# First merge stage: normalizers inverted as 8 columns a tile and spread over head dimensions on TensorE

## The reference

```
q = elu(q) + 1                                   # nodes x 8 x 64
k = elu(k) + 1
kv = einsum('bhnd,bhne->bhde', k, v)             # one 64x64 matrix a head
k_sum = sum(k over nodes)                        # one vector of 64 a head
out = einsum('bhnd,bhde->bhne', q, kv)
normalizer = einsum('bhnd,bhd->bhn', q, k_sum)   # one number a node and head
out = out / (normalizer[..., None] + 1e-8)
out = out.reshape(B, N, C) @ out_w.T + out_b
```

## Time and profile before

| what | value |
|---|---|
| time of the kernel, median of 3 runs | 4578.88 us (4555.28 to 4579.88) |
| span of the profiled execution | 4670.9 us |
| time outside that span | not shown by the profile |
| PE busy in the whole span | 4108.2 us (88%) |
| DVE busy | 3416.2 us (73%) |
| ACT busy | 2670.2 us (57%) |
| POOL busy | 2813.0 us (60%) |
| stage `merge0` | 1736 to 1960 us |

### The profile page before, as it was taken

One profiled execution on the slowest core, in us unless ns is written; L12 is line 12 of the kernel. 1 busy time (PEld: TensorE's weight loads), 2 busy tenths in 40 slices (PEclk: granted clock), 3 DMA queues, 4 the chain that ended last, 5 costly groups with the idle time before them and its releaser, 6 DMA issues. The chain is left out here.

```text
span 4670.9 us, 65873 instructions
## 1 busy us (share of the span) xinstructions
PE 4108.2 (88%) x16821; PEld 2295.3 (49%) x16821; DVE 3416.2 (73%) x9304; ACT 2670.2 (57%) x7162; POOL 2813.0 (60%) x2738
## 2 busy tenths in 40 slices
PE   7888888999999989979775889988889999999967
PEld 3344554555555545456454444444445555555543
DVE  8521226999999987667653888888888888888873
ACT  1111115888888871123254777777777777777720
POOL 1766664777777761013422777777777777777700
PEclk9988989999999999979887999999999999999978
DMA  4224115888888861257667999999999999988853
GB/s 178 89 96 138 37 37 179 255 257 256 252 256 255 253 214 59 83 190 232 194 210 248 223 223 225 221 228 225 223 230 222 222 224 222 224 218 217 181 167 134
DMA packets 368712, 910.65 MB, mean 195 GB/s; under 512 B 60879, under 2 KB 113086, under 8 KB 368089
## 3 DMA queue, kind: packets, MB, share of 16 engines
q0 software_dynamic: 209424, 663.87, 53.7%
q1 hardware_dynamic: 148287, 222.61, 14.4%
q10 hardware_dynamic: 10650, 20.19, 1.2%
HBM read 679.00 MB, written 227.92 MB: 194 GB/s over the span
## 5 line engine op out<-in xcount | busy, mean ns | idle before, releaser
L2126 POOL DMA_INDIRECT mid_acc<-m_out,m_il x416 | 688.4, 1655 | 149.9 <-issue 117.6
L2522 PE MATMUL m_pws<-m_w_s,m_hid 32*128 32x512 f32 x832 | 472.4, 650 | 138.9 <-DVE m_msg L2202 78.2
L2116 POOL DMA_INDIRECT m_drow<-mid_drow,m_ig x416 | 421.4, 1013 | 262.0 <-DMA m_ig<-in_gather_ix 111.8
L441 POOL DMA_INDIRECT mid_slots<-sort_rec,f_row x416 | 412.3, 991 | 264.8 <-issue 112.3
L807 POOL DMA_INDIRECT s_kv<-mid_kv_rows,keep_slot x440 | 425.9, 968 | 209.8 <-PE s_pm L1034 124.8
L1034 PE MATMUL s_pm<-s_kv,keep_free 128*128 128x260 f32 x1760 | 466.2, 388 | 47.5 <-ACT s_kv L951 37.5
L2530 PE MATMUL m_pm<-m_msg,m_same 128*128 128x512 f32 x832 | 491.4, 674 | 11.5 <-ACT m_out L2352 8.8
L2415 PEld LDWEIGHTS m_pip<-keep_ident,m_drow 128*128 128x128 f32 x2496 | 368.7, 204 | 246.3 <-issue 235.8
L2116 POOL DMA_INDIRECT m_srow<-mid_srow,m_ig x416 | 404.1, 971 | 126.9 <-issue 126.3
L2523 PE MATMUL m_pwf<-m_w_f,m_hid_f 32*128 32x512 f32 x832 | 476.7, 655 | 0.0
L1015 PE MATMUL s_pq<-queries_q,s_sameT 128*128 x880 | 467.8, 614 | 0.1
(11 more groups left out here) (396 smaller groups left out, 8619.1 us busy)
## 6 DMA issues: line engine op xcount, KB each, us to landing
mid_ys<-e_y SPq DMA_DIRECT2D x57, 256.0 KB
e_line<-in_src_lines POOLq DMA_DIRECT2D x52, 256.0 KB
m_line<-in_src_lines SPq DMA_DIRECT2D x104, 128.0 KB
m_xT<-mid_xhT SPq DMA_DIRECT2D x100, 128.0 KB
g_a<-mid_acc SPq DMA_DIRECT2D x50, 256.0 KB, 3.4
keep_w<-in_w SPq DMA_DIRECT2D x16, 512.0 KB
s_kv<-mid_kv_rows,keep_slot POOLq DMA_INDIRECT x440
mid_slots<-sort_rec,f_row POOLq DMA_INDIRECT x416
```

The lines of the kernel that those rows point to most:

```text
L441: pool.indirect_dma_start(io["slots"], bass.IndirectOffsetOnAxis(ap=sort.row[:, e:e + 1], axis=0), sort.rec[:, e, :], None,).then_inc(s_pu ...
L2116: pool.indirect_dma_start(row, None, table, bass.IndirectOffsetOnAxis(ap=ig[:, n, t:t + 1], axis=0),).then_inc(s_g[t % S], 16)
L2126: pool.indirect_dma_start(io["acc1"][k % NACC], bass.IndirectOffsetOnAxis(ap=il[:, t:t + 1], axis=0), out[:, k % R, :], None, compute_op=A ...
L2522: pe.matmul(pws[k % 2][:], hid[lanes, par, :], w_s2[lanes, :], start=True, stop=True)
```

## The change

- `keep.ksum` is now 2 columns a chunk, one for each head, instead of 128. VectorE writes it with 128x2 instructions.
- `head_sums` has its operands the other way round: q (128x128) is loaded and the 2 columns of `ksum` stream. The result is one number a node and head, nodes on the partitions: 8 columns a tile.
- ScalarE copies 8 columns, and VectorE inverts 8 columns (`inverses`).
- New is `spread_heads`: 8 products a tile. For head h, the column of inverses is loaded, repeated 64 times (128x64), and the identity streams with 128 columns. The result goes to 64 partitions of PSUM bank `pk`, partitions 0 to 63 for even h and 64 to 127 for odd h, turned as q is.
- VectorE multiplies q by that PSUM bank.
- Head sums, their copy and the inverses run two tiles ahead instead of one. Those of tiles 0 and 1 come before the folding. The spreading of tile 0 follows the folding and waits for all four copies of `kvw`; that of tile n+1 stands between the products of tile n with W and those with `kvw`.

```diff
-                    vec.tensor_tensor(keep.ksum[:, c, :].rearrange("p (h d) -> p h d", h=2),
-                                      pkv[:, c, P:P + 1].unsqueeze(2).broadcast_to([P, 2, DH]), over_dims(half), ALU.mult)
+                    vec.tensor_tensor(keep.ksum[:, c, :], pkv[:, c, P:P + 1].broadcast_to([P, 2]), half[:], ALU.mult)
...
 def head_sums(pe, q, ksum, bank):
     for c in range(KC):
-        cols = slice(P * c, P * (c + 1))
-        ins = pe.matmul(bank[:, cols], ksum[:, c, :], q[:, cols], start=True, stop=True)
+        ins = pe.matmul(bank[:, 2 * c:2 * c + 2], q[:, P * c:P * (c + 1)], ksum[:, c, :], start=True, stop=True)
+    return ins
+
+def spread_heads(pe, z, ident, bank):
+    for h in range(H):
+        rows, cols = slice(DH * (h % 2), DH * (h % 2 + 1)), slice(P * (h // 2), P * (h // 2 + 1))
+        ins = pe.matmul(bank[rows, cols], z[:, h:h + 1].broadcast_to([P, DH]), ident[:], start=True, stop=True)
     return ins
...
-        z, zq = s.sb("z", [P, 2, H]), s.sb("zq", [P, 2, D])
+        z, zq = s.sb("z", [P, 2, H]), s.sb("zq", [P, 2, H])
...
 # VectorE
-                def divide_queries(i, j):
-                    n = U * i + j
+                def inverses(n):
                     vec.wait_ge(s_zq, n + 1)
                     vec.reciprocal(zq[:, n % 2, :], zq[:, n % 2, :]).then_inc(s_rq, 1)
-                    vec.wait_ge(s_rq, n + 1)
-                    vec.tensor_tensor(q[:, j, :], q[:, j, :], zq[:, n % 2, :], ALU.mult).then_inc(s_q, 1)
+
+                def divide_queries(n):
+                    vec.wait_ge(s_spread, n + 1)
+                    vec.tensor_tensor(q[:, n % U, :], q[:, n % U, :], pk[n % 2][:], ALU.mult).then_inc(s_q, 1)
...
                 norm_edges(0, 0)
+                inverses(0)
+                inverses(1)
                 norm_edges(0, 1)
-                divide_queries(0, 0)
+                divide_queries(0)
 ...
-                        if not (isinstance(n, int) and n + 2 >= NT):
+                        if n + 2 < NT:
+                            inverses(n + 2)
                             norm_edges(i + (j + 2) // U, (j + 2) % U)
                         if not last_tile(n):
-                            divide_queries(i + (j + 1) // U, (j + 1) % U)
+                            divide_queries(n + 1)
                         add(i, j)
...
 # ScalarE
-                    need(act, s_q, n - 1)
-                    act.activation(zq[:, n % 2, :], pn[n % 2][:], ACT.Copy, bias=1e-8).then_inc(s_zq, 1)
+                    need(act, s_spread, n - 1)
+                    act.activation(zq[:, n % 2, :], pn[n % 2][:, 0:H], ACT.Copy, bias=1e-8).then_inc(s_zq, 1)
...
 # TensorE
+                def spread(n):
+                    pe.wait_ge(s_rq, n + 1)
+                    pe.wait_ge(s_kvw, KC)
+                    need(pe, s_q, n - 1)
+                    spread_heads(pe, zq[:, n % 2, :], keep.ident, pk[n % 2]).then_inc(s_spread, 1)
...
-                sums(0, 0)
+                sums(0)
+                sums(1)
                 turn(0, 0)
...
                     pe.matmul(pk[c % 2][:], kvT[:, P * c:P * (c + 1)], w_out[:, c, :], start=True, stop=True).then_inc(s_kw, 1)
+                spread(0)
...
+                        if n + 2 < NT:
+                            sums(n + 2)
                         if not last_tile(n):
-                            sums(*nxt)
                             turn(*nxt)
                         pe.wait_ge(s_aT, n + 1)
                         need(pe, s_x, n - 1)
                         for c in range(KC):
                             pe.matmul(pout[n % 2][:], aT[:, j, P * c:P * (c + 1)], W[:, c, :], start=c == 0, stop=False)
+                        if not last_tile(n):
+                            spread(n + 1)
                         pe.wait_ge(s_q, n + 1)
-                        if n == 0:
-                            pe.wait_ge(s_kvw, KC)
```

More of the change, by code:

```diff
@@ L1103, in merge0 @@
         s_back = [s.sem(f"x_back{j}") for j in range(U)]
-        s_st, s_agg, s_pn, s_zq, s_rq, s_q, s_ta, s_aT, s_mm, s_x = (s.sem(n) for n in (
-            "edge_steps", "edges", "head_sums", "normalizers", "inverses", "queries", "edgesT", "aT", "products", "x"))
+        s_st, s_agg, s_pn, s_zq, s_rq, s_spread, s_q, s_ta, s_aT, s_mm, s_x = (s.sem(n) for n in (
+            "edge_steps", "edges", "head_sums", "normalizers", "inverses", "inverses_spread", "queries", "edgesT", "aT", "products", "x"))
         s_kv, s_kvT, s_kw, s_kvw = (s.sem(n) for n in ("kv_turned", "kvT", "folded", "folded_weights"))
@@ L1185, in _, with normalizers @@
                 act.dma_start(W[:], io["w_ff"].rearrange("(c p) n -> p c n", p=P)).then_inc(s_w, 16)
-                def normalizers(i, j):
-                    n = U * i + j
+                def normalizers(n):
                     act.wait_ge(s_pn, n + 1)
-                    need(act, s_q, n - 1)
-                    act.activation(zq[:, n % 2, :], pn[n % 2][:], ACT.Copy, bias=1e-8).then_inc(s_zq, 1)
+                    need(act, s_spread, n - 1)
+                    act.activation(zq[:, n % 2, :], pn[n % 2][:, 0:H], ACT.Copy, bias=1e-8).then_inc(s_zq, 1)
                 def turned(i, j):
@@ L1200, in _ @@
                 act.activation(kvT[:], pk[1][:], ACT.Copy).then_inc(s_kvT, 1)
-                normalizers(0, 0)
+                normalizers(0)
+                normalizers(1)
                 turned(0, 0)
@@ L1208, in body @@
                     for j in range(U):
+                        n = U * i + j
                         nxt = (i + (j + 1) // U, (j + 1) % U)
-                        if not last_tile(U * i + j):
-                            normalizers(*nxt)
+                        if n + 2 < NT:
+                            normalizers(n + 2)
+                        if not last_tile(n):
                             turned(*nxt)
@@ L1216, in _, with sums @@
             def _(pe):
-                def sums(i, j):
-                    n = U * i + j
-                    pe.wait_ge(s_in[j], 16 * (i + 1))
+                def sums(n):
+                    pe.wait_ge(s_in[n % U], 16 * (n // U + 1))
                     need(pe, s_zq, n - 1)
-                    head_sums(pe, q[:, j, :], keep.ksum, pn[n % 2]).then_inc(s_pn, 1)
+                    head_sums(pe, q[:, n % U, :], keep.ksum, pn[n % 2]).then_inc(s_pn, 1)
+                def spread(n):
[3 more added lines that the diff above has]
+                    spread_heads(pe, zq[:, n % 2, :], keep.ident, pk[n % 2]).then_inc(s_spread, 1)
                 def turn(i, j):
@@ L2853, in program @@
         with Stage(nc, "keep0") as s0:
-            keep.kv, keep.ksum = s0.sb("kv", [P, KC, P]), s0.sb("ksum", [P, KC, P])
+            keep.kv, keep.ksum = s0.sb("kv", [P, KC, P]), s0.sb("ksum", [P, KC, 2])
             keep.slot, keep.loc, keep.owner = s0.sb("slot", [P, ST, 2], I32), s0.sb("loc", [P, ST]), s0.sb("owner", [1, ST], I32)
```

## The result

| | kernel before | changed kernel |
|---|---|---|
| median | 4573.28 us (9 runs, 4555.28 to 4579.88) | 4589.06 us (9 runs, 4581.37 to 4609.01) |
| ratio | | 1.0043, 95% interval 1.0025 to 1.0062 |
| span of the profiled execution | 4670.9 us | 4587.3 us |
| merge stage, first instruction to first of the next stage | 223.9 us | 254.5 us |

The change makes the kernel slower by 16 us (difference of the medians) to 20 us (the ratio), where 30 were forecast. The two profiled spans point the other way, and say nothing: the profile of before had spent 87 us more in the first stage than any of the other eleven (table under e6). So the comparison is made stage by stage.

The account below looks back on a forecast made before the run. The prediction took PE (TensorE) to bound the merge stage. Spreading 25 x 1.23 = 30.8 us, - 0.9 + 0.7 - 0.4, gave +30 us on 4578.9: 4609 us, with 8 in 10 between 4583 and 4636.

Parts of the forecast that it names:

- rival (c): Head sums: the load doesn't set the step, a 2-column record costs some 0.03 us; +15 us, 4594; chance 0.12.
- (b): Spreading: no products run side by side, 2.11 us a tile; +52 us, 4631; chance 0.15.
- (d): Spreading streams in its neighbours' shadow, costing PE at most what head sums give back; -11 us, 4568; chance 0.07.
- PE bounds the stage, the reciprocal is worth 0: Merge stage: PE has no gap, so VectorE's 3.1 us a tile saved on the reciprocal gain 0.
- Head sums stay at 0.88 us: Head sums on PE: the 128-column load sets the step, 8 x 0.11 = 0.88 us a tile, no saving.
- Spreading 1.23 us a tile: New PE step: 8 rounds 0.86, layout change 0.35, first loads 0.02 us, all added to the tile's period.
- The start of the stage: First spreading waits for folding's last copy: PE stands 0.80 us, 0.7 counted; tile 1's early head sums save 0.9.
- rival (e): Granted clock falls to 1.2 GHz for a third of the stage: +78 us more, 4690; chance 0.04.
- The sum: Whole kernel: 30.8 - 0.9 + 0.7 - 0.4 gives +30 us, the same added to the timed median.

Follow-up runs that it names:

- e6: Changed kernel with ksum kept at 128 columns a chunk (old SBUF layout), against the kernel before: ratio 1.0048, stage 253.5 us; stage and clock tables stand there.
- e4: Kernel before with only the first 8 of 512 columns inverted a tile, against the kernel before: ratio 0.9999, stage 224.9 us.
- e3: Changed kernel without the spreading of tiles 2 to 24, against the kernel before: ratio 1.0002, stage 225.5 us, period 8.15 us.
- e8: Changed kernel with the eight spreading products issued three times over, against the kernel before: ratio 1.0146, stage 297.4 us.
- e2: Changed kernel with inverses repeated by VectorE and spread by four 128-column products, against the kernel before: ratio 1.0033, stage 246.9 us, period 9.05 us.
- e7: Changed kernel with the four spreading products for partitions 0 to 63 first, then those for 64 to 127, against the kernel before: ratio 1.0081, stage 265.7 us.
- e5: Kernel before, unedited, run against itself as a control: ratio 0.9999.
- e1: Changed kernel again, unedited, against the kernel before: ratio 1.0053, stage 254.7 us.
- e9: Kernel before with head sums, their copy and the wide inverses two tiles ahead, no spreading, against the kernel before: ratio 1.0012, stage 222.8 us.

## Why the prediction was right, and where it was off

The time fell into the stated range, 4583 to 4636, but this is in part luck. By the number alone, 4589 lies outside the forecast's own range of 4596 to 4622 and nearer to rival (c), 4594. It is the tile's period, 9.37 us where the forecast had 9.43, (b) 10.3, (c) 8.8 and (d) 8.2 or less, that decides for the forecast's mechanism. Of the 20 us between 4609 and 4589, 6 are the kernel before, whose median came to 4573.3 in nine executions after 4578.9 in three; 14 are the change's own difference.

- **PE bounds the stage, the reciprocal is worth 0**: right, and shown by e4 (period 8.20 with VectorE at 3.1 us) and by e3.
- **Head sums stay at 0.88 us**: right within 0.07. 2 columns behind a load of 128 cost 0.81 us for eight records, 0.11 for each but the first, so rival (c) with 0.03 a record is out. Only the first record, whose load runs beside the wide products, takes 0.03 us.
- **Spreading 1.23 us a tile**: 1.22 (e3). Both parts hold: 0.87 in 8 rounds (e8), and for the layout 0.35 (the rest) or 0.32 (e2), where I had 0.86 and 0.35 from one passage of another stage. Rival (b) needs an order that the change doesn't have, and even then comes out at little more than half its price (0.49 of 0.88 us a tile, e7). Rival (d) would need the layout change hidden; it isn't.
- **The start of the stage**: PE stands 0.78 us for ScalarE's copy, forecast 0.80. The two are not counted alike: from the last column of the folding, as in the forecast, it is 0.94, of which 0.14 pass between the copy's end and the first narrow record. I had not seen that the queries of tile 1 arrive late: PE waits 2.98 us for them before its head sums. That lies in the wait for the weights, which ends 12.8 us after the stage's start as before (12.6), so it costs nothing. The folding's records took 6.17 us instead of 5.19, but 6.49 in e5, the kernel before, too: the granted clock rises at another moment in each execution, here between 1657 and 1660 us, in the kernel before between 1751.8 and 1754.3 us, and the mean clock over the folding was 0.58 here, 0.72 there and 0.55 in e5.
- **Clock**: 1.00 throughout the middle; rival (e) is out.
- **The sum**: the stage was forecast 30.6 us longer (the 30.2 of the sum, without the 0.4 that the first stage saves) and is 28.8 to 30.0 us longer than 224.7. The step that was off is the last: "the stage has no gather whose time could differ, so I add the same 30 us". The timed runs say +20, +24 and +22. The stage's difference holds at equal granted clock (27.5 and 27.6 us in e1 and e6), but the forecast had no term for the mean clock of the whole, which was 0.0013 to 0.0018 higher in those runs and gave back 4 to 6 us. In the first comparison the clocks of the kernel before are not on record, so its 10 us can't be divided in this way. Because of that the result fell inside 0.5%, for which I gave 0.25, and not over it, for which I gave 0.72. With a forecast that close to the bound, the chances should have counted an offset of 5 to 10 us between one stage and the whole.
- **Against what execution**: the first profile was 92 us over the median by its first stage, 718.8 against 627 to 632 us in all eleven others. Adding the difference to the timed median, and not to the span, was right for that reason; I had not named the place.

## What to carry to other kernels

Before moving work from a vector engine to TensorE, look which of the two has no gap between its records: here 3.1 us a tile were taken from an engine that waited, and 1.2 us given to the one that didn't. A product costs by its load as much as by its stream, so turning operands round to stream 2 columns instead of 128 gains next to nothing (0.05 us a tile) if 128 must be loaded each time; rounding both operands to bf16, half the records, does gain. That it is the load, and not another fixed cost of such a record, no run tells apart. When a timed difference and that of a stage disagree by a few us, the granted clocks of the compared executions are the first thing to lay side by side. Narrow products should alternate their output partitions and stand together in one run, since the layout is paid by the run.

## What the runs showed that was not expected

- Eight narrow products (16 records) cost 1.51 us with the places one after the other and 1.03 us alternating (e7). The upper half's first record started beside the lower half's fifth, three records ahead of its turn and not more.
- The VectorE multiply of the queries took 688 ns with one operand in PSUM. With both in SBUF it took 1142 ns on average in the kernel before, but 682 to 687 ns for 24 of 25 in e9, where its place in time was another, and 691 to 693 in e4. Record by record the difference is the time beside POOL's addition to the features:

```profile
1800.69 1.26 POOL L1132 TENSOR_TENSOR keep_x<-keep_x,g_extra 128x512 f32<-128x512 f32 x1 [7.16 <-DMA keep_x<-mid_x]
1801.24 1.26 DVE L1158 TENSOR_TENSOR g_q<-g_q,g_zq 128x512 f32<-128x512 f32 x1
```

  POOL ends at 1801.95, and the multiply 0.55 us later. Of the 25 multiplies of before, 22 overlap that addition, by 486 to 853 ns, and each lasts its overlap plus 0.55 us. So does the one of e9 that overlaps it, 794 ns with 247 of overlap. Of the three that don't, two take 691 and 692 ns, and the third, 986 ns, runs beside another addition of POOL's (L1128). In the changed kernel 20 of 25 run beside the same addition for their whole length and still take 686 to 690 ns, so with an operand in PSUM that cost doesn't arise. None of this was on the path here.
- Timed differences of a kernel with one stage altered lay up to 10 us from that stage's own difference, to both sides, with intervals that reach 6 to 13 us to either side. At the same granted clock they lay within 3 us (table under e6).
